# Stage one of a two-stage float32r kernel: the high weights times low x as a matmul of its own

## The reference

```python
y = einsum('bsi,boi->bso', x, weight[ids])                  # stage one, 1024 x 1024 per element
base_out = einsum('btd,od->bto', y, base_W) + base_b        # stage two from here
logits   = einsum('btd,nd->btn', y, router_W) + router_b    # 15 outputs
w        = top-8 softmax probabilities, put on their experts
h        = einsum('btd,erd->bter', y, A)                    # 8 experts, rank 16
out      = x + base_out + einsum('bter,eor->bto', h * w, B) * 2
```

## Time and profile before

| | |
|---|---|
| median of 3 runs | 422.23 us |
| the profiled execution, first to last instruction (span) | 421.1 us |
| mean granted TensorE clock | 0.996 of full speed |
| chain that ended last | PE 95%, DMA 2%, DVE 1% |
| matmuls and weight loads | 2356 each |
| stage one's split chunks | 62 (6 + 7 x 8), 8 values of k each: 496 of L546, 496 of L548 |

### The profile page before, as it was taken

The page is one execution under the profiler, slowest core; times in us unless marked ns, Lnnn a source line. Parts: engine busy times, 40 slices in busy tenths (PEclk is TensorE's granted clock), DMA queues, the critical chain, the costliest instruction groups (busy, mean ns, idle before and its releaser), DMA issues.

```text
span 421.1 us, 6443 instructions
## 1 busy us (share of the span) xinstructions
PE 413.3 (98%) x2356; PEld 390.4 (93%) x2356; DVE 220.0 (52%) x438; ACT 135.3 (32%) x236; POOL 0.8 (0%) x8
## 2 busy tenths in 40 slices
PE   6989999999999999999999999999999999999997
PEld 5879998899988999899998999989998899988996
DVE  2577858654266623676227652366424655255232
ACT  3475534630055300561015600365004540053000
POOL 0000000000000000000000000000000000000000
PEclk8999999999999999999999999999999999999999
DMA  6876966930177203771057511574016740150002
GB/s 201 287 281 215 362 238 255 339 128 0 69 252 283 95 0 121 270 256 50 0 191 269 196 42 50 194 280 173 0 50 224 280 144 0 50 199 2 0 2 100
DMA packets 20093, 64.72 MB, mean 154 GB/s; under 512 B 2418, under 2 KB 6130, under 8 KB 19186
## 3 DMA queue, kind: packets, MB, share of 16 engines
q1 hardware_dynamic: 20082, 64.57, 43.4%
HBM read 56.18 MB, written 8.39 MB: 153 GB/s over the span
## 4 chain that ended last, share of the span: by engine, by line
PE 95%; DMA 2%; DVE 1%; SPq 0%; ACT 0%; issue 0%
PE y_ps L546 26%; PE s_ps L578 16%; PE s_ps L577 16%; PE s_ps L580 16%; PE y_ps L548 13%; DMA w_raw<-in_wT 2%; PE y_ps L560 2%; PE s_ps L589 2%; PE s_ps L588 2%; PE s_ps L590 2%; PE s_ps L605 0%; DVE w_lo L385 0%; ACT s_hi L285 0%; SPq L195 0%; SPq L191 0%
## 5 line engine op out<-in xcount | busy, mean ns | idle before, releaser
L546 PE MATMUL y_ps<-x_split,w_hi 128*128 128x512 f32 x496 | 172.7, 392 | 1.2 <-DVE w_lo L385 1.2
L548 PE MATMUL y_ps<-x_split,w_lo 128*128 128x256 f32 x496 | 139.1, 280 | 0.0
L577 PE MATMUL s_ps<-s_hi,y_hi 128*128 128x392 f32 (+1 forms) x384 | 131.2, 342 | 0.0
L578 PE MATMUL s_ps<-s_lo,y_hi 128*128 128x392 f32 (+1 forms) x384 | 130.4, 340 | 0.0
L580 PE MATMUL s_ps<-s_hi,y_lo 128*128 128x392 f32 (+1 forms) x384 | 130.0, 339 | 0.0
L546 PEld LDWEIGHTS y_ps<-x_split,w_hi 128*128 128x128 f32 x496 | 92.9, 187 | 21.6 <-DVE w_lo L385 1.5
L548 PEld LDWEIGHTS y_ps<-x_split,w_lo 128*128 128x128 f32 x496 | 94.0, 190 | 0.0
L385 DVE TENSOR_TENSOR w_lo<-w_raw,w_hi 128x1024 fp32r<-128x1024 f32 x62 | 75.2, 1215 | 1.4 <-ACT w_hi L293 1.4
L577 PEld LDWEIGHTS s_ps<-s_hi,y_hi 128*128 128x128 f32 x384 | 72.2, 188 | 0.3
L578 PEld LDWEIGHTS s_ps<-s_lo,y_hi 128*128 128x128 f32 x384 | 72.2, 188 | 0.0
L580 PEld LDWEIGHTS s_ps<-s_hi,y_lo 128*128 128x128 f32 x384 | 72.1, 188 | 0.0
(11 more groups left out here) (46 smaller groups left out, 162.5 us busy)
## 6 DMA issues: line engine op xcount, KB each, us to landing
w_raw<-in_wT SPq DMA_DIRECT2D x63, 512.0 KB, 3.5
res<-in_x SPq DMA_DIRECT2D x16, 512.0 KB, 4.9
out<-res SPq DMA_DIRECT2D x15, 512.0 KB, 2.7
x_raw<-in_xT SPq DMA_DIRECT2D x7, 1024.0 KB, 5.5
c_raw<-in_base_t SPq DMA_DIRECT2D x8, 392.0 KB, 3.7
x_raw<-in_xT SPq DMA_DIRECT2D x4, 256.0 KB, 4.2
c_raw<-in_base_t SPq DMA_DIRECT2D x2, 480.0 KB, 7.4
w_raw<-in_wT SPq DMA_DIRECT2D x4, 128.0 KB, 4.4
```

The costliest lines, as they stand in the source:

```text
L546: nc.tensor.matmul(y_ps[:, o % 2, :], w_hi[:, slot, k, :], x_split[:, k, :, :].rearrange("p s t -> p (s t)"), start=(k == 0), stop=False)
L548: mm = nc.tensor.matmul(y_ps[:, o % 2, 0:T], w_lo[:, slot, k, :], x_split[:, k, 0, :], start=False, stop=(k == KC - 1))
L577: nc.tensor.matmul(dst, hi, s2_hi[:, k, cols], start=(k == 0), stop=False)
L578: nc.tensor.matmul(dst, hi, s2_lo[:, k, cols], start=False, stop=False)
```

## The change

The x tile is divided into `x_hi` and `x_lo`. Each k in stage one now has three matmuls of 256 columns, all into PSUM columns 0 to 255: w_hi*x_hi, w_hi*x_lo, w_lo*x_hi. The copy `y_part` and the addition `y_sum` are gone with their tiles and semaphores (and the two plain copies for the first element's chunks 0 and 1). ACT rounds `y_hi` straight from `y_ps`, and DVE makes `y_lo` straight from `y_ps` and `y_hi`. PE's wait for the bank of chunk o - 2 is now a wait on `y_lo` in place of `y_sum`. In the lists of ACT and DVE, what stood between y_part and y_hi, or between y_sum and y_lo, now stands behind y_hi or y_lo.

```diff
@@ scalar @@
-            def make_y_part(b, o, first=False):
-
+            def make_y_hi(b, o, first=False):
                 act.wait_ge(y_ps_done, OC * b + o + 1)
-                if not first or o >= F32_CHUNKS + 2:
-                    act.wait_ge(y_sum_done, OC * b + o - 1)
-                nc.scalar.copy(y_part[:, o % 2, :], y_ps[:, o % 2, T:2 * T]).then_inc(y_part_done, 1)
-
-            def make_y_hi(b, o, first=False):
-                act.wait_ge(y_sum_done, OC * b + o + 1)
                 if o == 0 and not first:
                     act.wait_ge(y_free, b)
-                nc.scalar.copy(y_hi[:, o, :], y_sum[:, o % 2, :]).then_inc(y_hi_done, 1)
+                nc.scalar.copy(y_hi[:, o, :], y_ps[:, o % 2, 0:T]).then_inc(y_hi_done, 1)
...
             def element(b, last=False):
                 for o in range(OC):
-                    make_y_part(b, o)
-                    more = not last or o + W_SLOTS < OC
-                    if more and o < OC - 1:
-                        adapter_hi(b, o + W_SLOTS)
                     make_y_hi(b, o)
-                    if more and o == OC - 1:
+                    if not last or o + W_SLOTS < OC:
                         adapter_hi(b, o + W_SLOTS)
@@ vector @@
             def make_y_lo(b, o):
                 dve.wait_ge(y_hi_done, OC * b + o + 1)
-                nc.vector.tensor_tensor(y_lo[:, o, :], y_sum[:, o % 2, :], y_hi[:, o, :],
+                nc.vector.tensor_tensor(y_lo[:, o, :], y_ps[:, o % 2, 0:T], y_hi[:, o, :],
                                         ALU.subtract).then_inc(y_lo_done, 1)
...
-            def make_y_sum(b, o):
-                dve.wait_ge(y_part_done, split(b, o))
-                nc.vector.tensor_tensor(y_sum[:, o % 2, :], y_ps[:, o % 2, 0:T], y_part[:, o % 2, :],
-                                        ALU.add).then_inc(y_sum_done, 1)
...
             for o, (before, after) in enumerate(steps):
-                if o < F32_CHUNKS:
-                    dve.wait_ge(y_ps_done, o + 1)
-                    nc.vector.tensor_copy(y_sum[:, o, :], y_ps[:, o, 0:T]).then_inc(y_sum_done, 1)
-                else:
-                    make_y_sum(0, o)
+                make_y_lo(0, o)
                 split_lo(before)
-                make_y_lo(0, o)
                 split_lo(after)
@@ tensor @@
                 pe.wait_ge(w_lo_done, split(b, o))
-                pe.wait_ge(y_sum_done, OC * b + o - 1)
+                pe.wait_ge(y_lo_done, OC * b + o - 1)
                 for k in range(KC):
-                    nc.tensor.matmul(y_ps[:, o % 2, :], w_hi[:, slot, k, :],
-                                     x_split[:, k, :, :].rearrange("p s t -> p (s t)"), start=(k == 0), stop=False)
-                    mm = nc.tensor.matmul(y_ps[:, o % 2, 0:T], w_lo[:, slot, k, :], x_split[:, k, 0, :],
+                    nc.tensor.matmul(y_ps[:, o % 2, 0:T], w_hi[:, slot, k, :], x_hi[:, k, :], start=(k == 0), stop=False)
+                    nc.tensor.matmul(y_ps[:, o % 2, 0:T], w_hi[:, slot, k, :], x_lo[:, k, :], start=False, stop=False)
+                    mm = nc.tensor.matmul(y_ps[:, o % 2, 0:T], w_lo[:, slot, k, :], x_hi[:, k, :],
                                           start=False, stop=(k == KC - 1))
                 mm.then_inc(y_ps_done, 1)
```

More of the change, by code:

```diff
@@ L74, in adaln_ffn_kernel @@
         x_raw = sb("x_raw", [P, KC, T])
-        x_split = sb("x_split", [P, KC, 2, T], F32R)
-        y_part = sb("y_part", [P, 2, T])
-        y_sum = sb("y_sum", [P, 2, T])
+        x_hi = sb("x_hi", [P, KC, T], F32R)
+        x_lo = sb("x_lo", [P, KC, T], F32R)
         y_hi = sb("y_hi", [P, KC, T], F32R)
@@ L138, in adaln_ffn_kernel @@
         y_ps_done = sem("y_ps_done")
-        y_part_done = sem("y_part_done")
-        y_sum_done = sem("y_sum_done")
         y_hi_done = sem("y_hi_done")
@@ L293, in adapter_hi, with make_x_hi @@
                 nc.scalar.copy(w_hi[:, slot, :, :], w_raw[:, slot, :, :]).then_inc(w_hi_done, 1)
[L295 removed]
+            def make_y_hi(b, o, first=False):
                 act.wait_ge(y_ps_done, OC * b + o + 1)
[L298 to L303 removed]
                 if o == 0 and not first:
                     act.wait_ge(y_free, b)
[L306 to L308 removed]
+                nc.scalar.copy(y_hi[:, o, :], y_ps[:, o % 2, 0:T]).then_inc(y_hi_done, 1)
+            def make_x_hi(b):
                 act.wait_ge(x_in, 16 * (b + 1))
@@ L312, in x_hi @@
                     k = slice(g * KC // 2, (g + 1) * KC // 2)
-                    nc.scalar.copy(x_split[:, k, 0, :], x_raw[:, k, :]).then_inc(x_hi_done, 1)
+                    nc.scalar.copy(x_hi[:, k, :], x_raw[:, k, :]).then_inc(x_hi_done, 1)
             def exponential(b):
@@ L324, in element @@
                 for o in range(OC):
-                    make_y_part(b, o)
-                    more = not last or o + W_SLOTS < OC
-                    if more and o < OC - 1:
-                        adapter_hi(b, o + W_SLOTS)
                     make_y_hi(b, o)
-                    if more and o == OC - 1:
+                    if not last or o + W_SLOTS < OC:
                         adapter_hi(b, o + W_SLOTS)
                 if not last:
-                    x_hi(b)
+                    make_x_hi(b)
                 exponential(b)
@@ L340, in _ @@
                 act.wait_ge(x0_in[j], 16)
-                nc.scalar.copy(x_split[:, k, 0, :], x_raw[:, k, :]).then_inc(x0_hi_done, 1)
+                nc.scalar.copy(x_hi[:, k, :], x_raw[:, k, :]).then_inc(x0_hi_done, 1)
             make_y_hi(0, 0, first=True)
@@ L345, in _ @@
             for o in range(1, OC):
-                if o >= F32_CHUNKS:
-                    make_y_part(0, o, first=True)
-                if o < F32_CHUNKS:
-                    make_y_hi(0, o, first=True)
+                make_y_hi(0, o, first=True)
                 if o + 3 < OC:
@@ L363, in _ @@
             shared_hi(N_SHARED - 1)
-            x_hi(0)
+            make_x_hi(0)
             make_hwt_hi(0)
@@ L386, in adapter_lo, with make_x_lo @@
                                         ALU.subtract).then_inc(w_lo_done, 1)
-            def x_lo(b, g):
+            def make_x_lo(b, g):
                 k = slice(g * KC // 2, (g + 1) * KC // 2)
                 dve.wait_ge(x_hi_done, 2 * b + g + 1)
-                nc.vector.tensor_tensor(x_split[:, k, 1, :], x_raw[:, k, :], x_split[:, k, 0, :],
+                nc.vector.tensor_tensor(x_lo[:, k, :], x_raw[:, k, :], x_hi[:, k, :],
                                         ALU.subtract).then_inc(x_lo_done, 1)
@@ L464, in output @@
                                                 res[:, t, cols], ALU.add).then_inc(out_done, 1)
-            def make_y_sum(b, o):
-                dve.wait_ge(y_part_done, split(b, o))
-                nc.vector.tensor_tensor(y_sum[:, o % 2, :], y_ps[:, o % 2, 0:T], y_part[:, o % 2, :],
-                                        ALU.add).then_inc(y_sum_done, 1)
             def element(b, last=False):
                 for o in range(OC):
[L473 to L476, removed]
                     make_y_lo(b, o)
-                    if more and o == OC - 1:
+                    if not last or o + W_SLOTS - 1 < OC:
                         adapter_lo(b, o + W_SLOTS - 1)
                 if not last:
-                    x_lo(b, 0)
-                    x_lo(b, 1)
+                    make_x_lo(b, 0)
+                    make_x_lo(b, 1)
                 routing(b)
@@ L524, in _ @@
             shared_lo(N_SHARED - 1)
-            x_lo(0, 0)
+            make_x_lo(0, 0)
             make_hwt_lo(0)
-            x_lo(0, 1)
+            make_x_lo(0, 1)
             for o in range(OC, OC + W_SLOTS - 1):
```

1 line of the change is left out of this document (removed).

## The result

| | before | after |
|---|---|---|
| median of 6 runs each | 422.36 us | 428.37 us |
| after / before | | 1.0142, 95% interval 1.0117 to 1.0166 |
| span of the profiled execution | 421.1 us | 426.4 us |
| matmuls with their loads | 2356 | 2852 |

What follows compares the result with a forecast made beforehand. The prediction took PE's dense matmul stream as the bound. Third matmul 6.3 us minus 0.3 us for copy and addition gave +6.0 on 421.1, span 427.1, plus 1.1 for the median: 428.2 us, range 424.0 to 430.4.

Steps and rivals of the forecast that it cites:

- What bounds it: Whole kernel: PE's dense matmul stream; ACT and DVE wait for PE, so work taken from them alone buys nothing.
- The third matmul: Stage one: a third matmul per k adds a fixed cost of 13.4 ns, 6.3 us over 472 k.
- column rival: Stage one: extra time goes with columns; third matmul adds 3.1 to 4.5 ns per k; 423.4 to 424.0 us; chance 0.15.
- 472 of 496: Stage one, first element: growth of chunks 2 to 4 vanishes in PE's wait before chunk 5, leaving 472 k.
- Copy and addition, -0.3 us: First element: without them on ACT and DVE, chunk 5 starts 0.31 us earlier, at 25.68 us; in the loop they were hidden.
- y_lo(o - 2) as a new wait: Stage one: PE's wait costs nothing; y_lo(1) ends about 1.1 us after chunk 1 and is wanted 2.88 us after it.
- Stage two unchanged: Stage two: its matmuls of 392 columns should stay at 177.7 ns each.
- The sum: Whole kernel: 6.3 - 0.3 = +6.0 us on 421.1, a span of 427.1 us; 1.1 us more for the median, 428.2 us.
- The cheap repeat: Stage one: a matmul repeating its neighbour's weights has no fixed cost; a k stays at 347 ns; 421.9 us; chance 0.06.
- The loads: Stage one: weight loads become the bound; 528 us if they can't overlap, 430 to 434 us in mild form; chance 0.04.

Runs made afterwards that it cites:

- the split alone: Kernel before with w_hi times x_lo as its own matmul, still into PSUM columns 256 to 511, copy and addition kept: 429.23 us, ratio 1.014.

## Why the prediction was right, and where it was not

- **What bounds it.** Right. Taking out the copy and the addition alone gave no difference, the split alone gave the whole loss.
- **The third matmul.** Right in size: 13.4 ns per k forecast, 13.0 measured over the stage in the profile (23.03 against 22.20 us over 64 k). The step of the argument, that 13.4 ns are a cost per matmul that holds from 240 to 392 columns, held at 256. It holds as a sum only. In the earlier trace rows the pair's two distances are 0.23 and 0.12 us; averaged over the loop, the trace of before has 230.2 ns behind the 512 columns and 116.6 behind the 256, so 16.9 and 9.9 ns over the columns and not 13.4 each. Three times 116.6 is 349.8, the figure of the column rival; the average of the pair was the better guide, and why the 256-column matmuls come to 120 ns among themselves stays open. As a rule the cost per matmul is too wide: it breaks at 128 columns, where the floor of 111.5 ns sets the pace, and it is float32r's own cost.
- **472 of 496.** The 24 k that were to vanish in the wait before chunk 5 did so only by way of an early landing. In the profile after there was no wait left to vanish in. From its first split matmul to the start of element 1 the first element ran 45.94 us (15.84 to 61.78) against 46.95 (16.07 to 63.02). The growth of six chunks, 0.6 us, was more than paid. Before, the six chunks took 1.7 us more than 48 k at 346.9 ns (16.07 to 34.42), with the wait and the slower matmuls behind it. After, they took 0.1 us more than 48 k at 359.8 ns (15.84 to 33.18).
- **Copy and addition, -0.3 us.** The steps themselves came as worked out. From the landing at 20.41 in the profile after, ACT began y_hi(3) 1.91 us later (forecast 1.89) and DVE w_lo(5) 2.64 us later (forecast 2.63). But the landing they start from was taken as fixed at 21.78 and is not. Nothing measured shows the 0.3 us, and the term is smaller than the noise of the start. The nearest to it is another wait: with the split alone and an early landing, PE waited 0.3 us for y_sum before chunk 6.
- **y_lo(o - 2) as a new wait.** Right for the kernel after: no wait. In the run with 32 weight columns PE waited 0.2 us on y_lo once, when a late transfer of x for the output kept DVE busy past the start of element 1. DVE's list has y_lo where y_sum stood, so by the lists a late DVE would have held y_sum up in the same way.
- **Stage two unchanged.** Off by a little. The loop of an element takes 51.63 us against 50.70 (starts of elements 2 and 3: 113.42 and 165.05 after, 113.72 and 164.42 before). Stage one accounts for 0.83, so stage two grew by 0.10. Its 48 matmuls of 384 columns take 8.47 us (136.45 to 144.92) against 8.39, while the 392-column ones are the same to 0.02. That makes 0.7 us over seven elements that the forecast had not. The growth comes with the split: stage two of element 2 takes 28.60 us after and with the split alone (136.56 to 165.16), and 28.50 before and without the copy and the addition alone (135.59 to 164.09). How the split reaches into stage two stays open.
- **The sum.** Seven elements at +0.93 are 6.5 us. Element 1 started 1.24 us earlier than before (61.78 against 63.02), so the span is 5.3 us longer, not 6.0, and 426.4 us where 427.1 was forecast. The medians differ by 6.0. Part of this close agreement is luck. The forecast put the median 1.1 us above the profile's span, from one profile and the median of three runs. In every later run the time is 1.8 or 1.9 us above its own span. So a span 0.7 us too long met an addition 0.7 us too small. The 0.7 us of stage two and the 0.3 us of the start were outside the sum or unshown.
- **The rivals.** The column rival fell with 120 ns per matmul at 256 columns, 360 per k where it had 350. The cheap repeat fell with equal distances between the three. The loads were waved off too lightly: they did not bind here, but the margin was 8 ns of 120, and the matmuls 0.11 us apart stood on the floor itself. They were no proof of room below 0.11, and the load rows 0.10 apart were a single pair.

## What to carry to other kernels

When PE is dense, a matmul costs its columns and something more. Every matmul here had a load of its own, so what a second matmul on weights already loaded would cost was not measured. With float32r in this kernel that something is 13 ns on average at 256 columns and more, so a wide matmul with an extra copy and addition on idle engines beats two narrow ones without. Below about 236 columns (an estimate: where N/2.4 + 13.3 meets 111.5 ns; only 128 and 240 columns were seen) a float32r matmul with its load costs about 111.5 ns whatever it streams. In bfloat16 the same choice is worth 2.6 ns per k, and the extra work on ACT and DVE may then weigh more.

## What the runs showed of the hardware that I had not expected

- In a long row, float32r matmuls with 128 weight columns each come no faster than one in 111.5 ns. With bfloat16, matmuls of 128 columns stood 55.8 ns apart.
- The fixed cost per matmul in a dense stream is 13 ns on average with float32r and 2.5 ns with bfloat16, for the same columns at the same granted clock of 1.00. Weights and moving operand were changed together, so which of the two carries it was not separated.
- With one of three float32r matmuls loading 64 weight columns a k took 350.0 ns, with 32 it took 353.3, with 128 it took 359.8. With 64, the distances behind the other two matmuls shrank too.
- The landing of one 512 KB transfer in the first 25 us moved by 3 us from execution to execution. PE's wait before chunk 5 was between 0.0 and 1.7 us in the four profiles shown.
